# Two half-size units first, interleaved last units, and layer 1 in two DVE steps

## The reference, cut to what matters

```python
e = stack([tbl_f[ids[:, f]] for f in range(32)], axis=1)        # 1024 x 32 fields x 16
xk = e
for W in (W0, W1, W2):                                          # 32 x h x 64
    xk = relu(einsum('bmd,bhd,mhk->bkd', e, xk, W))             # 1024 x 64 x 16
    outs.append(sum(xk, axis=2))
z = concatenate([*outs, dense_ctx], axis=1)                     # 1024 x 208
h = maximum(z @ W_top1 + b_top1, 0)                             # 512
h = maximum(h @ W_top2 + b_top2, 0)                             # 256
y = h @ W_top3                                                  # 1024 x 1
```

## Time and profile before

| what | us |
| --- | --- |
| median of three runs | 680.73 (674.42 to 684.67) |
| the profiled execution, its own time | 675.9 |
| span of the profiled execution, first to last instruction | 674.0 |
| PE busy | 572.9 (85%) |
| DVE busy | 558.0 (83%) |
| POOL busy | 461.0 (68%) |
| ACT busy | 317.5 (47%) |

### The profile page before, as it was taken

One profiled execution on the slowest core, in us unless ns is written; L12 is line 12 of the kernel. 1 busy time (PEld: TensorE's weight loads), 2 busy tenths in 40 slices (PEclk: granted clock), 3 DMA queues, 4 the chain that ended last, 5 costly groups with the idle time before them and its releaser, 6 DMA issues.

```text
span 674.0 us, 7501 instructions
## 1 busy us (share of the span) xinstructions
PE 572.9 (85%) x2472; PEld 191.5 (28%) x2472; DVE 558.0 (83%) x231; ACT 317.5 (47%) x1311; POOL 461.0 (68%) x353
## 2 busy tenths in 40 slices
PE   0047599989989898989898989898998989895997
PEld 0002132333323232323232323232333423231332
DVE  0039798989999999999899999999998999996400
ACT  0031447364555646454646473746456464643031
POOL 5776484977878887878697979788887873443000
PEclk9998699899999899989999999999898999997999
DMA  3296685776757576767586777777685667570000
GB/s 91 65 353 218 261 300 230 271 286 254 298 223 298 223 248 253 255 256 283 214 301 241 276 282 273 285 270 287 244 311 201 248 241 309 206 243 0 1 0 0
DMA packets 32918, 153.35 MB, mean 228 GB/s; under 512 B 11600, under 2 KB 21584, under 8 KB 24816
## 3 DMA queue, kind: packets, MB, share of 16 engines
q1 hardware_dynamic: 22656, 149.31, 57.6%
q0 software_dynamic: 8192, 2.11, 2.6%
q10 hardware_dynamic: 2032, 1.46, 0.7%
HBM read 147.61 MB, written 5.25 MB: 227 GB/s over the span
## 4 chain that ended last, share of the span: by engine, by line
PE 52%; DVE 21%; DMA 11%; issue 6%; ACT 5%; SPq 3%; POOL 2%; ACTq 0%; DVEq 0%
PE acc L484 47%; DVE prod L341 19%; DMA spread<-x_scratch 6%; DMA x_scratch<-xt 4%; ACT x L392 4%; SPq L205 3%; POOL rows L295 2%; PE x L553 2%; PE x L542 1%; DVE z L353 1%; DVE xt L331 1%; DMA first<-x_scratch 1%; PE x L559 1%; PE x L546 0%; PE acc L542 0%
## 5 line engine op out<-in xcount | busy, mean ns | idle before, releaser
L341 DVE TENSOR_TENSOR prod<-spread,x 128x4096 f32<-128x4096 f32 (+2 forms) x179 | 531.1, 3022 | 47.7 <-ACT x L392 20.4
L484 PE MATMUL acc<-prod,w 128*64 128x512 f32 x1932 | 453.7, 617 | 95.1 <-DVE prod L341 89.5
L295 POOL DMA_INDIRECT rows<-table,idx x256 | 242.7, 948 | 79.0 <-issue 70.4
L307 POOL TENSOR_TENSOR prod_pool<-spread,x_pool 128x1024 f32<-128x1024 f32 x93 | 218.1, 2374 | 84.3 <-ACT x_pool L392 84.1
L484 PEld LDWEIGHTS acc<-prod,w 128*64 128x64 f32 x1932 | 147.8, 141 | 389.5 <-issue 351.7
L392 ACT ACTIVATE x<-acc 64x512 f32<-64x512 f32 x128 | 73.0, 570 | 79.0 <-PE acc L484 77.8
L407 ACT ACTIVATE relu_out<-acc 128x512 f32<-128x512 f32 x48 | 28.7, 597 | 157.3 <-PE acc L484 156.5
L400 ACT ACTIVATE relu_out<-relu_out 128x16 f32<-128x16 f32 x480 | 95.3, 200 | 0.5
L484 PE MATMUL acc<-prod_pool,w 128*64 128x512 f32 x372 | 90.9, 592 | 0.0
L400 ACT ACTIVATION_READ_ACCUMULATOR relu_out<-relu_out 128x1 f32 x480 | 89.8, 187 | 0.0
L392 ACT ACTIVATE x_pool<-acc 64x512 f32<-64x512 f32 x128 | 75.7, 591 | 1.9
(11 more groups left out here) (20 smaller groups left out, 26.9 us busy)
## 6 DMA issues: line engine op xcount, KB each, us to landing
spread<-x_scratch SPq DMA_DIRECT2D x63, 2048.0 KB, 9.3
first<-x_scratch SPq DMA_DIRECT2D x16, 512.0 KB
rows<-table,idx POOLq DMA_INDIRECT x256
x_scratch<-xt SPq DMA_DIRECT2D x64, 48.0 KB
spread<-x_scratch SPq DMA_DIRECT2D x4, 512.0 KB, 8.2
x_scratch<-xt SPq DMA_DIRECT2D x60, 32.0 KB
w<-w ACTq DMA_DIRECT2D x2, 512.0 KB, 5.7
spread<-wt SPq DMA_DIRECT2D x2, 384.0 KB, 4.4
```

Source lines behind the costliest of these rows:

```text
L295: nc.gpsimd.indirect_dma_start(rows[u % 2][:, j * D:(j + 1) * D], None, table, bass.IndirectOffsetOnAxis(ap=idx[:, u, j:j + 1], axis=0)).t ...
L307: nc.gpsimd.tensor_tensor(prod_pool[:, k % POOL_SLOTS, :], tiles(u, t, 1)[:, 0, :], x[:, :], ALU.mult).then_inc(pool_ready, 1)
L341: nc.vector.tensor_tensor(prod[:, at:at + count, :], tiles(u, t, count), x[:, :].rearrange("p (a n) -> p a n", a=1).to_broadcast([P, count ...
L484: last = nc.tensor.matmul(to[K * blk:K * blk + K, :], w, moving[:, blk * BLK:(blk + 1) * BLK], start=start, stop=stop)
```

## The change

- The batch becomes 17 units: units 0 and 1 hold 32 samples (512 columns), units 2 to 16 hold 64. A half unit has eight gathers of 128 rows (four field groups), and its stores, loads, multiplies, matmuls and copies are half as wide. Its stores are ten DMAs, for unit 0 five by SP and five by ACT.
- Ids and offsets come in two contiguous loads; ACT runs a one-element activation ahead of unit 0.
- In unit 0, and in layer 2 of unit 1, Pool multiplies no tiles. The transpose of unit 1 comes right behind layer 1 of unit 0, that of unit 2 behind the first step of layer 3 of unit 0. The three later groups of unit 0 are issued together.
- The last two units are interleaved on DVE and PE: the first two steps of layer 3 of unit 15, layer 2 of unit 16, the other two steps of layer 3 of unit 15, layer 3 of unit 16. Unit 16's x2 takes the buffers of x0 and of Pool's x1.
- Layer 1 of units 1 to 16 is two DVE steps of two tiles.
- In the tower's first product the full units are 480 columns a half, and the two half units come as extra matmuls of 32 columns, with 128 rows for the layers. The output leaves in four DMAs.

The diff, cut to its core (lines of `...` stand for what is left out):

```diff
+HALVES = 2
+UNITS = HALVES + (B - HALVES * S // 2) // S
+LAST = UNITS - 1
...
+def width(u):
+
+    return N // 2 if half(u) else N
...
-    return () if (layer, u) == (2, 0) else (5, 6, 7)
+    return () if (layer, u) in ((2, 0), (3, 0), (2, 1)) else (5, 6, 7)
...
     if layer == 1:
-        return ((0, 1), (1, 1), (2, 1), (3, 1)) if u == 0 else ((0, 4),)
+        return ((0, 1), (1, 1), (2, 1), (3, 1)) if u == 0 else ((0, 2), (2, 2))
...
+CUT = 2
+CUT_ORDER = ([("step", 0), ("step", 1), ("pool", 0), ("pool", 1), ("pool", 2)], [("step", 2), ("step", 3)])
...
+        def store_half(engine, u, f):
+            for copy in range(copies(u, f)):
+                to = scratch(u, J // 2 * f + M * copy)
+                to = bass.AP(tensor=to.tensor, offset=to.offset, ap=[[N // 8, 4], [N // 2, J // 2], [1, N // 8]])
+                engine.dma_start(to, xt[u % 2][32 * f:32 * f + 32, 0:N // 8]).then_inc(scratch_in[u % 2], 16)
...
             sp.wait_ge(turned, 1)
-            store(sp, 0, 0)
+            for f in range(0, 4, 2):
+                store_half(sp, 0, f)
             load_first(0)
             for t in range(G):
                 load(0, t, 1, tile_in[t])
 
             sp.wait_ge(tile_in[1], 16)
-            load_group(0, 1)
-            sp.wait_ge(tile_in[3], 16)
-            load_group(0, 2)
-            sp.wait_ge(*loaded(0, G))
-            load_group(0, 3)
+            for g in range(1, GROUPS):
+                load_group(0, g)
...
             turn(0)
             layer_1(0)
-            for u in range(UNITS):
+            turn(1)
+            for u in range(LAST):
                 dve.wait_ge(x_ready[0], u + 1)
                 for i in range(len(steps_of(2, u))):
                     multiply(2, u, i, x1)
-                    if u == 0 and i == 2:
-                        turn(1)
...
+            for i in range(CUT):
+                multiply(3, LAST - 1, i, x2)
+            sum_d(LAST - 1, 1)
+            dve.wait_ge(x_ready[0], LAST + 1)
+            for i in range(len(steps_of(2, LAST))):
+                multiply(2, LAST, i, x1)
+            sum_d(LAST, 0)
+            for i in range(CUT, len(steps_of(3, LAST - 1))):
+                multiply(3, LAST - 1, i, x2)
+            dve.wait_ge(x_ready[1], LAST + 1)
+            for i in range(len(steps_of(3, LAST))):
+                multiply(3, LAST, i, x2_of(LAST))
+                if i == 1:
+                    sum_d(LAST, 1)
+            sum_d(LAST, 2)
...
+            done = layer(LAST - 1, 3, CUT_ORDER[0])
+            layer(LAST, 2, order_of(2, LAST))
+            layer(LAST - 1, 3, CUT_ORDER[1], done)
+            layer(LAST, 3, order_of(3, LAST))
...
+                for g in range(HALVES):
+                    for l in range(3):
+                        nc.tensor.matmul(to_h1(t, g)[:, FULL:BLK], w_top1[:, l, t * P:(t + 1) * P],
+                                         z[:, l, z_at(g):z_at(g) + S // 2], start=l == 0, stop=False)
+                    own = slice(64 * g, 64 * g + D)
+                    nc.tensor.matmul(to_h1(t, g)[:, FULL:BLK], w_dense[own, t * P:(t + 1) * P], dense[own, FULL:BLK],
                                      start=False, stop=True).then_inc(h1_mm, 1)
```

More of the change, by code:

```diff
@@ L6 @@
 P = 128
-UNITS = 16
-S = B // UNITS
+S = 64
 N = S * D
@@ L32, with half, fields, copies @@
 MIDDLE = 11
+def half(u):
+    return u < HALVES
+def width(u):
+    return N // 2 if half(u) else N
+def fields(u):
+    return J // 2 if half(u) else J
+def copies(u, f):
+    return 3 if f * fields(u) < J else 2
+def stores(u):
+    return sum(copies(u, f) for f in range(4)) if half(u) else 8
+def z_at(u):
+    return FULL + u * S // 2 if half(u) else (u - HALVES) * S // 2
 def pool_tiles(layer, u):
-    return () if (layer, u) == (2, 0) else (5, 6, 7)
+    return () if (layer, u) in ((2, 0), (3, 0), (2, 1)) else (5, 6, 7)
 def steps_of(layer, u):
     if layer == 1:
-        return ((0, 1), (1, 1), (2, 1), (3, 1)) if u == 0 else ((0, 4),)
+        return ((0, 1), (1, 1), (2, 1), (3, 1)) if u == 0 else ((0, 2), (2, 2))
+    second = 1 if pool_tiles(layer, u) else 4
     if layer == 2:
-        return (0, 2), (2, 2), (4, 4 if u == 0 else 1), (8, 4), (12, 2), (14, 2)
-    return (0, 4), (4, 1), (8, 4), (12, 4)
+        return (0, 2), (2, 2), (4, second), (8, 4), (12, 2), (14, 2)
+    return (0, 4), (4, second), (8, 4), (12, 4)
 def order_of(layer, u):
@@ L89, with sequence, every @@
-PLACES, POOL_PLACES = places()
+CUT = 2
+CUT_ORDER = ([("step", 0), ("step", 1), ("pool", 0), ("pool", 1), ("pool", 2)], [("step", 2), ("step", 3)])
+def sequence():
+    def every(layer, u):
+        return [(layer, u, i) for i in range(len(steps_of(layer, u)))]
+    yield from every(1, 0)
+    for u in range(LAST):
+        yield from every(2, u)
+        yield from every(1, u + 1)
+        if u + 1 < LAST:
+            yield from every(3, u)
+    yield from every(3, LAST - 1)[:CUT]
+    yield from every(2, LAST)
+    yield from every(3, LAST - 1)[CUT:]
+    yield from every(3, LAST)
@@ new lines, in places, with pool_places @@
+def places():
+    out, owner, at, made = {}, [0] * RING, 0, 0
+    for number, (layer, u, i) in enumerate(sequence()):
+        count = steps_of(layer, u)[i][1]
+        if at + count > RING:
+            at = 0
+        out[layer, u, i] = number, at, max(owner[at:at + count]), made + count
+        for k in range(count):
+            made += 1
+            owner[at + k] = made
+        at += count
+    return out
+def pool_places():
+    order = [(layer, u) for u in range(LAST - 1) for layer in (2, 3)]
+    order += [(2, LAST - 1), (3, LAST - 1), (2, LAST), (3, LAST)]
+    tiles = [(layer, u, i) for layer, u in order for i in range(len(pool_tiles(layer, u)))]
+    return {tile: k for k, tile in enumerate(tiles)}
@@ L92, in made, with banks @@
+def banks():
+    order = [(1, 0)]
+    for u in range(LAST):
+        order += [(2, u), (1, u + 1), (3, u)]
+    order += [(2, LAST), (3, LAST)]
+    out, had = {}, {}
+    for n, stage in enumerate(order):
+        bank = out[2, LAST][0] if stage == (3, LAST) else n % 2
+        out[stage] = bank, had.get(bank)
+        had[bank] = stage
+    return out
+PLACES, POOL_PLACES, BANKS = places(), pool_places(), banks()
 def made(layer, u, i=-1):
@@ L183, in build, with gathers_done, stores_done @@
         y_mm, y_out, stored = sem("y_mm"), sem("y_out"), sem("stored")
+        def gathers_done(u):
+            return 16 * sum(fields(v) for v in range(u % 2, u + 1, 2))
+        def stores_done(u):
+            return 16 * sum(stores(v) for v in range(u % 2, u + 1, 2))
         def tiles(u, t, n):
@@ L449, in _ @@
             act.dma_start(w_top3[:, :], wt3.rearrange("(t p) o -> p (t o)", p=P), allow_slow_non_contiguous=True).then_inc(small_in, 16)
+            act.wait_ge(consts_in, 48)
+            nc.scalar.activation(warm[:, :], w_sq[0:1, 0:1], ACT.Relu)
             act.wait_ge(turned, 1)
-            store(act, 0, 1)
+            for f in range(1, 4, 2):
+                store_half(act, 0, f)
             base_tile(0)
```

332 lines of the change are left out of this document (173 added, 159 removed).

## The result

The changed kernel takes 686.97 us (median of four runs, 682.77 to 691.63), the kernel before 681.04 (674.42 to 684.67): a ratio of 1.0128, interval 1.0072 to 1.0185. It is slower by about 1.3%, less than 2%. The prediction was 666 us, in a range of 655 to 678: the sign is wrong and the time outside. Both profiled executions carry it: 675.9 us before, 685.45 after, spans 674.0 and 683.3.

A forecast was written before the change was run, and what follows sets the result against it. In the middle DVE and PE were both full, so only the ends could shrink. From 675.9 us: start -17.0, middle +2.7, end -5.4, tower +9.3 gave 665.5, so 666 us; range 655 to 678 for 8 in 10.

The forecast's parts named there:

- The waits ahead of layer 1: Start: three waits of layer 1 for transpose, stores and load, 1.6 us each, 4.8 in all.
- layer 3 of unit 2 after 105: Start: a sign that the prediction falls; it expected this stage to begin at 98.0, 17.0 us saved.
- the slow rival: Middle: transpose, stores and load set every period, 37.0 us; decides from 38.3, then 695 us; chance 0.05.
- DVE's 62.1 us of work: Start: DVE's stages from layer 2 of unit 0 up to layer 3 of unit 2, without waits.
- 64 short records and their row-group changes: Tower: 32-column matmuls at 0.107 us each, 6.8, plus 2.2 for row-group changes; tower 9.3 lost in all.
- The estimate of 1.6 us from the Trainium skill: Tower: 64 short matmuls at 25 ns each; the forecast sum would then be 660.
- The middle: 13 periods of 36.0 us, 468.0 in all, 2.7 more than before; bounds 35.3 and 36.9 a period.
- the split: Middle: layer 1 in two steps puts a 2.3 us PE gap ahead of layer 3; clock falls cost 0.57 a period.
- the split does nothing: Middle: rival that 465.3 us stays, gap included, giving 663; counted within the forecast's 0.50.
- The end: Last two units interleaved: 50.7 us instead of 56.1, 5.4 saved.
- the wait for the last group: End: layer 2 of unit 16 reaches the last loads early; 1.1 us of waiting, none to 4.
- half-size loads would be no faster: Start: rival with 5.4 us more at the load, up to 3 at copies, 671 to 676; slow start's chance 0.21.

The follow-up runs named there:

- e6_early: e2_fold with the transposes and stores of units 1 to 3 begun sooner and two output DMAs: 667.92 us, ratio 0.9786 to the kernel before.
- e2_fold: Changed kernel without short matmuls: ACT copies and DVE adds fold the half units' sums into the full-unit layout; 677.39 us, ratio 0.9901 to the kernel before.
- e3_short_last: Changed kernel with the tower's short matmuls all behind the four blocks of long ones: 693.49 us, ratio 1.0173 to the kernel before.
- e9_wide_128: Changed kernel with the tower's 64 short records 128 columns wide instead of 32, for time alone: 679.8 us, ratio 0.9982 to the kernel before.
- e8_after_again: The changed kernel itself, unaltered, run again as yardstick beside other runs: 691.5 us, ratio 1.0098 to the kernel before.
- e1_one_step: Changed kernel with layer 1 of later units in one DVE step of four tiles: 689.85 us, ratio 1.0101 to the kernel before.
- e7_early_one_step: e6_early with layer 1 of later units in one DVE step of four tiles: 668.31 us, ratio 0.9732 to the kernel before.
- e4_end_only: Kernel before with only the interleaved end, contiguous index loads and warm-up activation, sixteen units of 64: 677.1 us, ratio 0.9929.
- e5_act_stores: Changed kernel with the stores of every unit from 1 on shared between SP and ACT: 686.33 us, ratio 1.0053 to the kernel before.

## Why the prediction was wrong

**The waits ahead of layer 1: the step that failed most.** The prediction named the three places and took 1.6 us each, 4.8, from the 2.32 us of a full unit's late load. They came to 12.3, and with two small waits for PE and ACT behind them (0.54 and 1.23) to 14.1: 9.3 us of the 11.7 missed. The prediction's own sign of being wrong, layer 3 of unit 2 after 105, came true with 109.66. The chain was in the rows, 0.7 us from the transpose to the stores, 11.7 to the load's issue and 9.7 to landing: 22.1 us, where the three chains took 19.0, 21.0 and 22.1. I had set this sum up for the slow rival, in a full unit's 35 us where it fits, and not for the stages of the half units, where it doesn't: less the 13.4, 16.7 and 19.7 us that DVE had to lay over it in after, it gives waits of 8.7, 5.4 and 2.4, 16.5 in all for the 12.3 measured. The rest of the start was sized well: layer 2 of unit 0 came 2.0 us late (33.05 for 31.1), and DVE's 62.1 us of work are borne out by e6_early, where 34.03 + 62.1 and 5.8 us of waits give 101.9 and the row shows 102.70.

**The tower: a term without its second price.** 64 short records and their row-group changes were put at 9.0 us and measured 9.4. The sum was lucky in its parts: at full clock the records start 0.13 us apart (634.44 to 635.22 for six) and not 0.107, which leaves less than priced for the row group. What was missing is the clock: 6.1 us that the long matmuls pay. The prediction looked for the fall of the clock only behind idle gaps, and PE has none here. e2_fold shows the whole price, e3_short_last moves it, e9_wide_128 takes the clock's part away. The four output issues took 4.3 us (678.99 to 683.3) where 1.2 more than two was priced: as predicted. The estimate of 1.6 us from the Trainium skill (TensorEngine Tiling (Array Packing), section Instruction Overhead) doesn't hold here: at full clock the short records start 0.13 us apart, not 25 ns.

**The middle: a right number, and by luck in this execution.** 13 periods took 469.25 us against 468.0. The gap of 2.32 us in one piece ahead of layer 3 is there:

```profile
184.81 6.21 PE L608 MATMUL acc<-prod,w 128*64 128x512 f32 x20 [2.32 <-DVE prod L439]
...
221.15 4.51 PE L608 MATMUL acc<-prod,w 128*64 128x512 f32 x20 [2.51 <-DVE prod L439]
...
294.11 6.21 PE L608 MATMUL acc<-prod,w 128*64 128x512 f32 x20 [1.48 <-DVE prod L439]
```

But the clock fell only four times in fourteen, 4.2 us, where 7.4 were priced (13 times 0.57); it fell after 1.48 us and not after 2.51. Late loads held DVE up eight times, 0.39 to 4.25 us, 12.9 in all, partly hidden in the wait for x2; 1.3 were priced. Two errors cancelled. They are errors of this execution: in e8_after_again, the same kernel, the clock fell seven times in fourteen, about as often as priced, and in the other traces with two steps five to nine times. What is wrong in the term is its cause, the split: with one step, in e1_one_step and e7_early_one_step, the clock fell as often, eight times. For the rival "the split does nothing" speak these counts; the times neither show nor exclude the 2.7 us.

**The end** was right: 51.8 us for 50.7, and the wait for the last group, priced 1.1, was 2.07 (at 597.15). e4_end_only confirms its worth by itself.

**The rivals.** That half-size loads would be no faster gave 671 to 676: its direction was right, its place wrong, since it isn't the first load but the three chains behind it. None of the rivals held the tower's clock.

**Median and profile.** The prediction added up the profiled execution and left the sum for the median. The profiled run of before lies 5.1 us under its median, that of after 1.5: by the medians the change costs 5.9 us, by the spans 9.3.

**What stays open.** Why loads in the middle are late in some units and not in others, and so why the periods differ between kernels with the same middle: 35.8 us before, 36.1 after, 36.6 in e4_end_only, 36.4 in e6_early. e5_act_stores and e6_early suggest that the transfers in flight set how long a store takes to land; that was not tried by itself. Nor was it tried what sets where in the tower the clock falls.

## What to carry to other kernels

Cutting the first units in half shortens what scales with bytes and not the chain of transpose, store, wait and load: lay each chain against the work that stands beside it, and start it sooner, ahead of other loads, before you make the work smaller. A change that saves at one end can leave many small matmuls at the other; fold their operands together on other engines (e2_fold), and where they must stay, price the clock of what runs behind them too.

## What the runs showed of the hardware

PE's clock fell to 1.2 GHz while the profile shows PE busy 4.00 of 4.00 us: in after among sixteen 32-column records, in e3_short_last among 64 of them (0.50 from 650 to 662 us). With 128 columns a record it stayed at 1.00. The Trainium skill, TensorE: Matmul & The Clock Gate, section Why this matters for your kernels, advises padding for thin matmuls; the run with 128 columns agrees, at 24.7 us for 30.0, though here no wait for a DMA stood between the matmuls; the run with 256 kept the clock too and gained nothing, at 31.4.

A store's landing hardly hung on how it was issued: 10.3 us from the first store to the load with four issues on SP and four on ACT (e5_act_stores, unit 4), 10.1 with eight on SP (after, the same unit). In e5_act_stores and e6_early it went with what stood ahead of it: unit 1's load went after 11.3 us where the stores stood behind unit 0's later loads (e5_act_stores) and after 6.5 where they stood ahead of them (e6_early).
